# Another order of the opening of a two-layer gated attention kernel on one core

## The reference

```python
x = x + tanh(g_xattn[0]) * L0_xattn(layernorm(x), ctx)   # 16 heads of depth 8
x = x + tanh(g_ffn[0])   * L0_ffn(layernorm(x), weight)  # Hadamard, 4-bit activations, ternary weights
x = x + tanh(g_xattn[1]) * L1_xattn(layernorm(x), ctx)   # 16 heads of depth 64, masked
x = x + tanh(g_ffn[1])   * L1_ffn(layernorm(x), ...)     # 32 experts, top 4, capacity, and a shared one
```

## Time and profile before

| | |
|---|---|
| median of 3 runs | 272.05 us (271.31 to 272.85) |
| the profiled execution | 272.69 us, its span 270.7 us |
| TensorE busy | 252.7 us (93%) |
| VectorE busy | 212.8 us (79%) |
| ScalarE busy | 191.0 us (71%) |
| GpSimd busy | 181.0 us (67%) |

### The profile page before, as it was taken

The page is one execution under the profiler, slowest core; times in us unless marked ns, Lnnn a source line. Parts: engine busy times, 40 slices in busy tenths (PEclk is TensorE's granted clock), DMA queues, the critical chain, the costliest instruction groups (busy, mean ns, idle before and its releaser), DMA issues.

```text
span 270.7 us, 6704 instructions
## 1 busy us (share of the span) xinstructions
PE 252.7 (93%) x1903; PEld 199.6 (74%) x1903; DVE 212.8 (79%) x654; ACT 191.0 (71%) x454; POOL 181.0 (67%) x271
## 2 busy tenths in 40 slices
PE   7888999999788999989999999999989999979994
PEld 5655667776656777768777788877767778878993
DVE  3799998999999896799677877777798525885673
ACT  2587898998799777857776776777776563656562
POOL 7357999985879766746743595348848695836380
PEclk9999999999999999999999999999999999999998
DMA  6556573400024854644574757766532041201630
GB/s 198 193 176 240 202 236 115 121 0 4 1 53 105 179 126 98 145 89 108 143 208 105 191 158 187 185 160 180 128 90 61 25 137 39 93 27 43 199 97 19
DMA packets 25987, 32.91 MB, mean 122 GB/s; under 512 B 4000, under 2 KB 18144, under 8 KB 25824
## 3 DMA queue, kind: packets, MB, share of 16 engines
q1 hardware_dynamic: 25520, 32.27, 44.0%
q10 hardware_dynamic: 432, 0.22, 0.3%
HBM read 14.32 MB, written 3.47 MB: 66 GB/s over the span
## 4 chain that ended last, share of the span: by engine, by line
PE 58%; DVE 15%; POOL 10%; issue 10%; ACT 3%; SPq 1%; DMA 1%; DVEq 0%; POOLq 0%; ACTq 0%
PE bank L1248 13%; PE bank L1421 13%; PE bank L1383 5%; PE bank L1253 5%; PE bank L1384 5%; PE bank L1255 4%; PE bank L1254 4%; DVE masked L962 4%; POOL probs L623 3%; POOL q L667 3%; PE bank L1436 2%; DVE probsT L979 2%; PE bank L1444 1%; PE bank L1501 1%; PE bank L1377 1%
## 5 line engine op out<-in xcount | busy, mean ns | idle before, releaser
L623 POOL TENSOR_SCALAR probs<-probs,rsum 128x512 f32<-128x512 f32 x128 | 87.9, 693 | 53.9 <-DVE rsum L971 52.9
L766 ACT ACTIVATE probs<-masked,neg_max 128x512 f32<-128x512 f32 x128 | 91.7, 718 | 12.9 <-DVE neg_max L962 10.0
L1248 PE MATMUL bank<-ident,probs 128*128 128x128 f32 x512 | 78.5, 276 | 2.2 <-DVE probsT L979 0.9
L1248 PEld LDWEIGHTS bank<-ident,probs 128*128 128x128 f32 x512 | 58.6, 141 | 18.6 <-issue 10.2
L962 DVE CUSTOM_DVE_ANT_0 masked<-bank,mask 128x512 f32<-128x512 f32 x64 | 43.8, 685 | 15.3 <-PE bank L1384 14.7
L775 ACT ACTIVATE probsT<-bank 128x512 f32<-128x512 f32 x74 | 43.5, 588 | 16.0 <-PE bank L1248 15.6
L1421 PE MATMUL bank<-probsT,val 128*32 128x256 f32 (+1 forms) x512 | 46.6, 384 | 0.0
L962 DVE CUSTOM_DVE_ANT_0 masked<-bank,shared 128x512 f32<-128x512 f32 x64 | 43.4, 678 | 0.4 <-PE bank L1377 0.3
L979 DVE COPY probsT<-bank 128x512 f32<-128x512 f32 x54 | 36.8, 681 | 8.8 <-PE bank L1248 8.6
L1421 PEld LDWEIGHTS bank<-probsT,val 128*32 128x32 f32 (+1 forms) x512 | 24.4, 123 | 17.7 <-issue 4.4
L1377 PE MATMUL bank<-parts 128*128 128x512 f32 x64 | 31.2, 488 | 2.7 <-DVE neg_max L962 1.4
(11 more groups left out here) (238 smaller groups left out, 525.3 us busy)
## 6 DMA issues: line engine op xcount, KB each, us to landing
k_both<-k_low SPq DMA_DIRECT2D x32, 128.0 KB, 2.7
k_both<-k_high SPq DMA_DIRECT2D x32, 128.0 KB, 2.8
q<-q_split SPq DMA_DIRECT2D x32, 128.0 KB, 2.4
probsT<-staged_gate SPq DMA_DIRECT2D x32, 128.0 KB, 3.0
q<-q_split SPq DMA_DIRECT2D x32, 64.0 KB, 2.1
parts<-staged_k SPq DMA_DIRECT2D x7, 256.0 KB, 2.7
w_flat<-in_w SPq DMA_DIRECT2D x1, 1536.0 KB, 7.3
staged_k<-k_high SPq DMA_DIRECT2D x2, 512.0 KB, 3.1
```

What stands on the lines that cost most here:

```text
L623: pool.tensor_scalar(p, p, rsum[:, u % NCOL:u % NCOL + 1], 1.0, ALU.mult, ALU.mult).then_inc(normed, 1)
L766: act.activation(probs[:, u % NP, :], masked[:, u % NS, :], ACT.Exp, scale=-1.0, bias=neg_max[:, c:c + 1], accum_out=sums[:, c:c + 1]).the ...
L1248: ins = pe.transpose(dst[0:rows, t * P:t * P + P], src, ident[:, :])
```

## The change

- The order of the jobs becomes k, ln, q, kn, qn, on TensorE, ScalarE and VectorE.
- VectorE, not ScalarE, copies the transposed rows to `xnT` (`first_rows`).
- VectorE makes the ternary weights right behind the first norm: parts 0 and 1, then `first_rows`, then part 2, then k's sum and query0(0), and only then kn's part, mask_max(0), qn's part, query0(1), mask_max(1), query0(2), query0(3).
- GpSimd clears `q0[:,1]` alone ahead of the first norm. `q0[:,2:4]` is cleared behind the mask conversion, which now waits for the ternary weights rather than for `xn`. The waits on `late_ready` count one more.
- TensorE's fillers behind jobs: one behind ln, one behind qn; before it was one behind kn, one behind ln, two behind qn.

```diff
--- before.py
+++ after.py
@@ -121,7 +121,7 @@
 def make_plan():
 
 
-    before = [("k", 0), ("kn", 0), ("ln", 0, 0), ("q", 0), ("qn", 0)]
+    before = [("k", 0), ("ln", 0, 0), ("q", 0), ("kn", 0), ("qn", 0)]
     plan = {1: [("v0", 0)]}
     for k in BLOCKS[8:]:
         early = 1 if k.m == 10 else 0
@@ -522,8 +522,8 @@
 
             stage_k0(0)
             stage_q0(0)
-            sp.wait_ge(late_ready, 3)
             for k in BLOCKS[1:4]:
+                sp.wait_ge(late_ready, 3 if k.m == 1 else 4)
                 stack_k0(k)
                 stack_q0(k)
             sp.dma_start(m1_u8[:, :, :, :], a["mask1"]).then_inc(ld["m1"], 16)
@@ -670,14 +670,14 @@
             pool.memset(warm[:, :], 0.0).then_inc(warm_ready, 1)
             publish_late(pool.memset(val[:, 0, :, :], 0.0))
             publish_late(pool.memset(q0[:, 0, :, :].bitcast(F32), 0.0))
-            publish_late(pool.memset(q0[:, 1:4, :, :].bitcast(F32), 0.0))
+            publish_late(pool.memset(q0[:, 1, :, :].bitcast(F32), 0.0))
             pool.wait_ge(ld["cols"], 16)
             rstd_of(0, 0)
 
-            pool.wait_ge(xn_ready, NQ)
+            pool.wait_ge(fw_ready, 1)
             pool.wait_ge(ld["m0"], 16)
             pool.tensor_scalar(mask0[:, :, :], m0_u8[:, :, :], FAR, -FAR, ALU.mult, ALU.add).then_inc(mask_ready[0], 1)
-            pool.wait_ge(fw_ready, 1)
+            publish_late(pool.memset(q0[:, 2:4, :, :].bitcast(F32), 0.0))
             publish_late(pool.memset(val[:, 1:NV, :, :], 0.0))
 
             def values(b, g):
@@ -789,7 +789,7 @@
             def job(j):
 
                 name, n = j[0], NUMBER[j]
-                if name in ("v0", "v1", "ffn", "rank", "rotate", "out"):
+                if name in ("v0", "v1", "ffn", "rank", "rotate", "out") or j == ("ln", 0, 0):
                     return
                 job_bank, free = job_banks[PLACE[j][0]], job_free[PLACE[j][0]]
                 act.wait_ge(job_done, n + 1)
@@ -1018,8 +1018,6 @@
                             dve.scalar_tensor_tensor(out=k0[:, 0, :], in0=job_bank[:, :], scalar=bk00[:, 0:1], in1=high_k.bitcast(F32),
                                                      op0=ALU.add, op1=ALU.add).then_inc(free, 1)
                             return
-                        for h in range(2):
-                            query0(h)
                         return
                     dve.wait_ge(high_ready, HIGHS[j])
                     if name == "k":
@@ -1036,6 +1034,12 @@
                         low, bank_in, bias, high = q1_split[:, i, 1, :], job_bank[:, 0:SQ], bq1, q1_split[:, i, 0, :]
                     dve.scalar_tensor_tensor(out=low, in0=bank_in, scalar=bias[:, row], in1=high.bitcast(F32),
                                              op0=ALU.add, op1=ALU.subtract).then_inc(free, 1)
+
+            def first_rows():
+
+                j = ("ln", 0, 0)
+                dve.wait_ge(job_done, NUMBER[j] + 1)
+                dve.tensor_copy(xnT[:, 0, 0:SQ], job_banks[PLACE[j][0]][:, 0:SQ]).then_inc(job_free[PLACE[j][0]], 1)
 
             def query0(h):
 
@@ -1123,7 +1127,7 @@
                     dve.tensor_reduce(lg[:, :], logits, X, ALU.max, negate=True).then_inc(lmax_ready, 1)
                 if o == 8:
 
-                    dve.wait_ge(late_ready, 9)
+                    dve.wait_ge(late_ready, 10)
                     dve.wait_ge(*freed(("logits", b)))
                     step(dve.reciprocal(lr[:, :], ls[:, :]))
                     step(dve.tensor_tensor(sc[:, :, :], ex[:, :, :], lr[:, :].unsqueeze(2).to_broadcast([P, NQ, EXPERTS]), ALU.mult))
@@ -1160,17 +1164,21 @@
             for dst, bias, sign in ((minus_bk0, bk00, lo_k), (minus_bq0, bq00, lo_q)):
                 dve.tensor_scalar(dst[:, :], bias[:, :], sign[:, 0:1], None, ALU.mult).then_inc(minus_ready, 1)
             ln_norm(0, 0)
+            ternary(0)
+            ternary(1)
+            first_rows()
+            ternary(2)
             dve.wait_ge(late_ready, 2)
-            for j in BEFORE[:-1]:
-                job(j)
-                if j[0] == "kn":
-                    for part in range(3):
-                        ternary(part)
+            job(("k", 0))
+            dve.wait_ge(high_ready, HIGHS["q", 0])
+            query0(0)
+            job(("kn", 0))
             dve.wait_ge(mask_ready[0], 1)
             mask_max(0)
-            job(BEFORE[-1])
+            job(("qn", 0))
+            query0(1)
+            mask_max(1)
             query0(2)
-            mask_max(1)
             query0(3)
             for t in range(-LEAD, EXPERTS_AT):
                 if t + LEAD - 1 == TOTAL // 2:
@@ -1376,7 +1384,7 @@
                         pe.wait_ge(stacked0[k.m % 4], 80 * turns_of_stack0(k.m))
                     pe.matmul(dst, q0[:, k.m % 4, h, q], k0[:, k.m % 4, :], start=True, stop=True).then_inc(scored, 1)
                 else:
-                    pe.wait_ge(late_ready, 6)
+                    pe.wait_ge(late_ready, 7)
                     s = k.m % NKQ
                     pe.wait_ge(k_stacked[s], 64 * turns_of_stack(k.m))
                     pe.wait_ge(q_stacked[s], 64 * turns_of_stack(k.m))
@@ -1449,7 +1457,7 @@
                 if j[0] == "ln":
                     pe.wait_ge(ld["ident"], 16)
                 job(j)
-                keep_busy({"kn": 1, "ln": 1, "qn": 2}.get(j[0], 0))
+                keep_busy({"ln": 1, "qn": 1}.get(j[0], 0))
             def attend(t):
 
                 if 0 <= t + LEAD < TOTAL:
```

## The result

The changed kernel is slower: 274.0 us median of 20 executions (272.77 to 275.65) against 272.1 of the kernel before (271.13 to 274.16, 20), a ratio of 1.0061 with an interval of 1.0045 to 1.0077, so 1.2 to 2.1 us. The forecast was 272.3 within 271.1 to 273.5.

What follows compares the result with a forecast made beforehand. It took the kernel as a mostly TensorE-bound pipeline gated by its start; the front's 0.92 us gain was held up by SyncE's staging, mask_max(8) came 0.2 later, so 272.1 became 272.3 us, range 271.1 to 273.5.

Steps and rivals of the forecast that it cites:

- Front: Opening on all engines: `veps` stall gone, query0(0) at 8.95 not 10.87, mask_max(0) 1.41 us earlier, kn's low part 1.48 later.
- SyncE, up to stack_q: SyncE staging through DRAM: keys out 1.48 us later, queries landing behind them near 16.7, stack_q 0.35 to 0.5 later.
- first rival: Block 1's scores can start by 18.8, so the front's 0.92 us gain carries through: 271.1 us; chance 0.13.
- Scores of block 1 start at 19.9: TensorE, block 1: scores end at 20.37 and mask_max(8) starts at 20.43, 0.2 us later than before.
- the slack of 0.29: Block 1's scores ended at 19.95 and mask_max(8) started at 20.24, leaving SyncE's branch 0.29 us to VectorE.
- third rival: TensorE falls to the 1.2 GHz level after its wait for block 1's scores: +3, 275.3 us; chance 0.04.
- The idle time: TensorE's wait for block 1's scores, scores(8): about 1.9 us instead of 0.55.
- second rival: SyncE's stage_k: the staging delay of 1.48 passes on whole, less 0.29 slack: +1.2, 273.2 us; chance 0.14.
- faster by over 0.5%: Whole kernel faster by more than 0.5% (1.36 us), needing the first rival and a coupling on top: chance 0.11.
- a coupling on top: A later coupling between GpSimd and VectorE, of the kind `veps` shows, adding to the first rival's gain; no size given.
- the rest: Shifts that later couplings between GpSimd and VectorE add or take, either way: chance 0.07.

Runs made afterwards that it cites:

- e1: The changed kernel measured again without edit, beside the kernel before: 273.39 us, ratio 1.0055.
- g1: The changed kernel with ScalarE, not VectorE, copying the transposed rows: 272.92 us, ratio 1.0022 to the kernel before.
- g2: The kernel before with 24 already met waits on VectorE ahead of the first norm: 273.14 us, ratio 1.0035.
- f1: The kernel before with only SyncE's key staging waiting in addition for ScalarE's qn part: 273.04 us, ratio 1.0007.
- e2: The changed kernel with four TensorE fillers ahead of scores(8), inside its wait: 273.76 us, ratio 1.0063 to the kernel before.
- f3: The kernel before with the smaller early clear and all three ternary parts right behind the first norm: 272.14 us, ratio 0.9976.
- f2: The kernel before with only SyncE's key staging waiting in addition for mask_max(0): 274.9 us, ratio 1.0083.

## Why the prediction was wrong

- **Front: right.** The clear, the transposes, the ternary parts, `first_rows` (0.42, forecast 0.41), query0 and kn's delay (1.57 in e1, at equal pace of TensorE, forecast 1.48) came as worked out.
- **SyncE, up to stack_q: right.** 16.92 in e1, forecast about 16.7 plus a little. The queries did land behind the keys (14.97 and 16.51 in the first profile), and stack_q did not go out by 15.7, which the first rival needed.
- **The failed step:** "Scores of block 1 start at 19.9". It carried over the old distance between stack_q and scores(8), 3.13, as if it belonged to the transfers. It was 3.73, since VectorE's instruction fetch had moved from 22 to 19 us, into the last query transfers, of which one part in 16 then landed 0.51 us behind the rest. g1 and g2 show this from both sides. The prediction has no term for such a fetch. With stack_q 0.57 later and the distance 0.60 longer, less the slack of 0.29, mask_max(8) would be 0.9 later; 1.21 was measured in e1, with scores(8) itself 0.30 slower at the low clock.
- **The third rival** was given 0.04 and +3. It happened in 22 of 31 executions of the changed kernel, at about 0.65 each by the estimate above, 0.45 in the mean. The idle time was forecast at 1.9 us and was 2.6.
- **The second rival** gave 273.2 and had 0.14; its size is near by luck, its mechanism is not what happened: f1 shows that the plain delay of staging is mostly absorbed.
- **The sum as shown:** 0.9 by stack_q and the distance, 0.45 by the clock in the mean, is 1.35, inside the 1.2 to 2.1 measured, at its lower end.
- **The chances:** faster by over 0.5% was given 0.11 although it needed the first rival (0.13) and a coupling on top (from the rest's 0.07) at once; by its own figures it should have been far less. It did not come to bear.
- **Still open:** the held part is seen in four profiles out of four with the fetch in that place, but the records do not say which DMA engine moved it or the fetch; that both sat on one engine is likely and not shown. Why e2's part was 0.86 behind and the others 0.51 to 0.60 isn't known. Each distance is from one profile. g1's median lies 0.9 us or more under the changed kernel's where 0.5 of distance went, and g2 lost 0.9 where the distance grew by 0.67; fewer low clocks (2 of 12) are a part in g1, the rest isn't explained, and later fetches moved too.

## What to carry to other kernels

Follow a reordered job to what is queued behind its output, and when a branch has 0.3 us of slack, price the wait at its end, what the idle engine does afterwards (here the clock), and not only the issue. A landing time read in one trace holds only beside the same traffic. Added or removed instructions on VectorE moved its instruction fetch here, so look where q14 falls before and after, and whether one part of a transfer lands behind the rest. Where a transfer decided, fewer bytes helped more than any order: keys written once took 0.9% off the changed kernel. On f3, where it hardly decided, they took off nothing that can be told.

## What the runs showed of the hardware

- 24 already met waits on VectorE, in its idle time, moved an instruction fetch from 22 to 18 us; the kernel was 0.35% slower (272 us).
- With the fetch among four 32 KB reads, one of the last read's 16 parts landed 0.51 to 0.86 us behind the others (four profiles); without it, at most 0.04 (ten profiles).
- The granted clock fell to 0.50 after TensorE had idled 2.64 us in e1 and stayed at 1.00 after 2.63 in the profile of the same program; 14 of 20 and 8 of 11 executions show the lower mean. In f2 two 512-column matmuls behind 3.15 us of idling still took 0.48 and 0.49 us, and only the third, at 23.37, took 0.78.
- The two records of TensorE's first 512-column product took 1.02 to 1.99 us together from one profile to the next at about the same start (4.82 to 5.06), so fronts of two profiles are to be compared only after setting that off.
